# A one-core cross-attention and feed-forward kernel: the attention stage written out with paired score banks, shared rings and more DMA moves

## The reference, cut to what matters

```python
# B = 16 batches, 128 channels, T = 512; 8 heads of 16 channels, 8 of them rotary
x = x + tanh(g_xattn) * attention(layernorm(x), ctx)
x = x + tanh(g_ffn)   * ffn(layernorm(x))

def attention(x, c):
    q, k, v = Wq @ x + bq, Wk @ c + bk, Wv @ c + bv      # per batch, 128 x 512
    q, k = rope(q), rope(k)                              # first 8 channels of each head
    scores = einsum('bhqd,bhkd->bhqk', q, k) / sqrt(16)  # 512 x 512 for each head
    return Wo @ (softmax(scores) @ v) + bo

def ffn(x):                                              # weights packed in 4 bits with scales
    gate, up = x @ w_gu.T                                # 2 x 1408 wide
    y = (silu(gate) * up) @ w_down.T
    return y / rms(y)
```

## Time and profile before

| what | value |
|---|---|
| median of 3 executions | 930.14 us (928.13 to 931.05) |
| the profiled execution | 933.48 us, its span 931.6 us |
| mean granted TensorE clock in it | 0.94 of full |
| PE busy | 840.4 us (90%), 4134 matmuls |
| DVE busy | 557.3 us (60%) |
| ACT busy | 527.6 us (57%) |
| POOL busy | 211.5 us (23%) |
| DMA | 45439 packets, 74.36 MB |

### The profile page before, as it was taken

The page is one execution under the profiler, slowest core; times in us unless marked ns, Lnnn a source line. Parts: engine busy times, 40 slices in busy tenths (PEclk is TensorE's granted clock), DMA queues, the critical chain, the costliest instruction groups (busy, mean ns, idle before and its releaser), DMA issues. The chain is left out here.

```text
span 931.6 us, 13887 instructions
## 1 busy us (share of the span) xinstructions
PE 840.4 (90%) x4134; PEld 419.6 (45%) x4134; DVE 557.3 (60%) x1024; ACT 527.6 (57%) x991; POOL 211.5 (23%) x194
## 2 busy tenths in 40 slices
PE   4689989899898999998897579999999999999997
PEld 1333333333333333333321466666666666666664
DVE  5778988788988988889971872313231323232113
ACT  3228878788888888887874553325232523252223
POOL 5202434333434433341221940000000000000000
PEclk9559989999999999999966879999999999999999
DMA  6564453454554455443200101000200020000001
GB/s 187 147 184 124 127 151 112 146 160 130 154 153 123 152 147 164 129 133 86 70 24 12 57 1 46 1 0 22 69 1 1 15 75 0 0 11 34 1 1 45
DMA packets 45439, 74.36 MB, mean 80 GB/s; under 512 B 12122, under 2 KB 14426, under 8 KB 45402
## 3 DMA queue, kind: packets, MB, share of 16 engines
q1 hardware_dynamic: 45402, 73.90, 26.6%
HBM read 48.17 MB, written 25.17 MB: 79 GB/s over the span
## 5 line engine op out<-in xcount | busy, mean ns | idle before, releaser
L648 DVE TENSOR_REDUCE row_max<-s_ps 128x1 f32<-128x512 f32 x512 | 320.2, 680 | 54.1 <-PE s_ps L367 52.7
L540 ACT ACTIVATE probs<-st_ps 128x512 f32<-128x512 f32 x512 | 271.7, 599 | 97.3 <-PE st_ps L420 95.7
L367 PE MATMUL s_ps<-k_stack,q_stack 48*128 48x512 f32 x512 | 211.3, 489 | 24.9 <-DMA k_stack<-qk_scratch 21.4
L420 PE MATMUL st_ps<-q_stack,k_stack 50*128 50x512 f32 x512 | 197.2, 479 | 24.7 <-ACT probs L540 19.5
L367 PEld LDWEIGHTS s_ps<-k_stack,q_stack 48*128 48x128 f32 x512 | 91.7, 196 | 175.8 <-DVE row_max L648 126.8
L1123 PE MATMUL gu_ps<-x_head,gu_head 128*128 128x512 f32 x352 | 156.0, 443 | 0.0
L979 DVE TENSOR_TENSOR hidden<-gu_ps,silu 128x512 f32<-128x512 f32 x44 | 30.4, 690 | 202.6 <-ACT silu L1062 202.6
L388 PE MATMUL pv_ps<-probs,v_ones 128*32 128x512 f32 x1024 | 144.8, 640 | 0.0
L1062 ACT ACTIVATE silu<-gu_ps 128x512 f32<-128x512 f32 x44 | 26.3, 597 | 204.8 <-PE gu_ps L1126 204.7
L1124 PE MATMUL gu_ps<-x_rest,gu_head 128*128 128x512 f32 x352 | 138.9, 395 | 0.0
L420 PEld LDWEIGHTS st_ps<-q_stack,k_stack 50*128 50x128 f32 x512 | 82.9, 194 | 79.2 <-ACT probs L540 59.7
(11 more groups left out here) (131 smaller groups left out, 928.2 us busy)
## 6 DMA issues: line engine op xcount, KB each, us to landing
qk_scratch<-split SPq DMA_DIRECT2D x32, 512.0 KB, 4.5
k_stack<-qk_scratch SPq DMA_DIRECT2D x192, 64.0 KB, 2.2
q_stack<-qk_scratch SPq DMA_DIRECT2D x64, 128.0 KB, 2.5
xt<-x_dram SPq DMA_DIRECT2D x16, 256.0 KB, 2.9
ct<-ctx_dram SPq DMA_DIRECT2D x16, 256.0 KB, 3.7
cv<-ctx_dram SPq DMA_DIRECT2D x16, 256.0 KB, 2.8
q_stack<-qk_scratch SPq DMA_DIRECT2D x64, 64.0 KB, 2.5
x_res<-x_dram SPq DMA_DIRECT2D x16, 256.0 KB, 4.9
```

What stands on the lines that cost most here:

```text
L367: nc.tensor.matmul(s_ps[n % RING][:], q_stack[p][rows, head // 2, qt * P:(qt + 1) * P], k_stack[p][rows, head // 2, :], start=True, stop=T ...
L420: nc.tensor.matmul(st_ps[n % RING][:], k_stack[p][rows, head // 2, kt * P:(kt + 1) * P], q_stack[p][rows, head // 2, :], start=True, stop= ...
L540: nc.scalar.activation(probs[unit % 2][:, head % QUAD, kt % 2], st_ps[n % RING][:], ACT.Exp).then_inc(expd, 1)
L648: nc.vector.tensor_reduce(row_max[p][:, head % 2, head // 2, qt:qt + 1], s_ps[n % RING][:], AXIS_X, ALU.max).then_inc(maxed, 1)
```

## The change

The attention stage is written anew. All loops are unrolled, the weight stage of feed-forward too.

- **Scores:** the two heads at partition 0 and 64 write one double bank (`s_ps`, two of [128, 2, 512]), and one reduction takes both maxima, already negated. Both scores of a slot stand ahead of its two transposed scores.
- **Rings:** `misc_ps` is gone. Mixing (slot 1 of 16, for batch b-2), the rotary projection (slot 2) and the other (slot 5, both for b+3) take their turn in the three `st_ps` banks; the values projection takes a score bank (slot 8, after the scores). The exponentials write three `probs` tiles of one kt each; the values products stay in odd slots.
- **Maxima:** turned by a 32 x 32 transpose on DVE (`turn_max`), stored to DRAM and loaded into the stack in halves (`store_max`, `load_max`).
- **Rotary partners:** four SBUF to SBUF transfers (`swap_partners`) in place of the shuffle.
- **Sums:** two transfers gather the sums of a batch (`gather_sums`), DVE takes the reciprocal of a [128, 32] tile (`invert_sums`), and two transfers store it and one spreads it (`store_inverse`, `load_inverse`); four more put both quads into one tile (`merge_quads`), so that one multiplication on POOL scales all heads (`scale_heads`).
- **Moved:** the head parts go from ACT to DVE (`head_pass`, `head_rot`), `normalise` from DVE to POOL; x stays in eight tiles and ctx in four, so neither is loaded twice; `load_half` is four transfers from an image in DRAM that four stores for each half of the channels write. SP issues 38 transfers for a batch.
- **Feed-forward:** the unpacked 8-bit numbers are read as they are by `scale_tile`; the conversion to bf16 (`gu_vals`, `dn_vals`) is gone. The unpacking stands in the last step.

The diff, cut to its core:

```diff
-UNITS = 4
-RING = 3
+ST_BANKS, S_BANKS = 3, 2
+X_TILES, C_TILES, PROBS = 8, 4, 3
+MIX_AT, ROT_AT, PASS_AT, V_AT = 1, 2, 5, 8
...
-        s_ps = [ps(f"s_ps{r}", [P, T], F32) for r in range(RING)]
+        s_ps = [ps(f"s_ps{r}", [P, 2, T], F32) for r in range(S_BANKS)]
         pv_ps = ps("pv_ps", [P, T], F32)
-        misc_ps = ps("misc_ps", [P, T], F32)
...
+            def swap_partners(sp, n):
+                sp.wait_ge(st_read, ST_NO["rot", n] + 1)
+                if n:
+                    sp.wait_ge(rot_rest, n)
+                for at in range(0, P, 64):
+                    for to, source in ((at, at + 32), (at + 32, at)):
+                        sp.dma_start(swap[to:to + 32, :], proj[source:source + 32, 0, :]).then_inc(swapped, 16)
...
+            def load_max(sp, n, h):
+                sp.wait_ge(max_out[h], 16 * (n + 1))
+                for odd in two:
+                    row = STACK * odd + DATA_ROWS
+                    sp.dma_start(q_stack[n % 2][row:row + MAX_ROWS, columns(h), :].bitcast(F32).rearrange("r j t -> r (j t)"),
+                                 max_dram[n, h, :, odd].rearrange("r i e -> r (i e)")).then_inc(max_in[n % 2][h], 16)
...
+            def sync_step(sp, b):
+                nxt, proj_n = b + 1 < B, b + AHEAD_PROJ
+                if nxt:
+                    load_half(sp, b + 1, 1)
+                store_max(sp, b, 1)
+                if proj_n < B:
+                    swap_partners(sp, proj_n)
+                if b:
+                    gather_sums(sp, b - 1, 1)
+                    merge_quads(sp, b - 1)
+                load_max(sp, b, 1)
+                if b >= 2:
+                    store_x(sp, b - 2)
+                if b:
+                    store_inverse(sp, b - 1)
+                if proj_n < B:
+                    store_head(sp, proj_n, 1)
+                if b + 2 < B:
+                    load_half(sp, b + 2, 0)
+                if nxt:
+                    store_max(sp, b + 1, 0)
+                if b:
+                    load_inverse(sp, b - 1)
+                if proj_n < B:
+                    store_rest(sp, proj_n, 1)
+                if b + 5 < B:
+                    load_inputs(sp, b + 5)
+                if nxt:
+                    load_max(sp, b + 1, 0)
+                gather_sums(sp, b, 0)
+                if proj_n < B:
+                    store_head(sp, proj_n, 0)
+                    store_rest(sp, proj_n, 0)
...
+            def st_bank(pe, item):
+                n = ST_NO[item]
+                if n >= ST_BANKS:
+                    pe.wait_ge(st_read, n - ST_BANKS + 1)
+                return st_ps[n % ST_BANKS]
...
+            def tensor_step(pe, b):
+                for slot in range(SLOTS):
+                    if b + 1 < B:
+                        score(pe, b + 1, slot)
+                        if slot == V_AT:
                             project_v(pe, b + 1)
+                    weigh(pe, b, slot)
+                    if slot == MIX_AT and b >= 2:
+                        mix(pe, b - 2)
+                    if slot == ROT_AT and b + AHEAD_PROJ < B:
+                        project_rot(pe, b + AHEAD_PROJ)
+                    if slot == PASS_AT and b + AHEAD_PROJ < B:
+                        project_pass(pe, b + AHEAD_PROJ)
+                    if slot >= 3 and slot % 2:
+                        values(pe, b, slot // 2 - 1)
+                    elif slot == 1 and b:
+                        values(pe, b - 1, SPANS - 1)
...
+            def scalar_step(act, b):
+                for slot in range(SLOTS):
+                    for odd in two:
+                        exponential(act, b, 2 * slot + odd)
+                    if slot == MIX_AT and b >= 2:
+                        gate(act, b - 2)
+                    if slot == ROT_AT and b:
+                        values_out(act, b - 1, 1)
+                    if slot == ROT_AT and b + AHEAD_PROJ < B:
+                        bias_rot(act, b + AHEAD_PROJ)
+                    if slot == PASS_AT and b + AHEAD_PROJ < B:
+                        bias_pass(act, b + AHEAD_PROJ)
+                    if slot == 7 and b + 4 < B:
+                        inverse_dev(act, b + 4)
+                    if slot == 10:
+                        values_out(act, b, 0)
...
+            def maxima(dve, n, slot):
+                item = S_NO["score", n, slot]
+                j, qt = score_of(slot)
+                dve.wait_ge(s_full, item + 1)
+                nc.vector.tensor_reduce(neg_max[j // 2][:, :, j % 2, qt], s_ps[item % S_BANKS][:], AXIS_X, ALU.max,
+                                        negate=True).then_inc(s_read, 1)
...
+            def vector_step(dve, b):
+                proj_n = b + AHEAD_PROJ
+                for slot in range(SLOTS):
+                    if b + 1 < B:
+                        maxima(dve, b + 1, slot)
+                        if slot == V_AT:
+                            take_v(dve, b + 1)
...
+                    if slot == 0:
+                        turn_max(dve, b, 1)
+                    if slot == 3 and b + 4 < B:
+                        statistics(dve, b + 4)
+                    if slot == 6 and b:
+                        invert_sums(dve, b - 1)
+                    if slot == 7 and b + 1 < B:
+                        turn_max(dve, b + 1, 0)
+                    if slot == 7 and proj_n < B:
+                        head_pass(dve, proj_n)
+                    if slot == 11 and proj_n < B:
+                        head_rot(dve, proj_n)
...
-                for b in two:
-                    tensor_step(pe, b, b, B - 1 - b)
-                with pe.Fori(1, B // 2 - 2) as i:
-                    for p in two:
-                        tensor_step(pe, i * 2 + p, p, 4)
-                for b in range(B - 4, B):
-                    tensor_step(pe, b, b % 2, B - 1 - b)
+                for b in range(B):
+                    tensor_step(pe, b)
...
             def source(t):
+            parts = [keep[name][:].bitcast(FP8E3) for name in ("part_a", "part_b")]
```

1047 lines of the change are left out of this document (474 added, 573 removed).

## The result

The changed kernel takes 938.97 us (median of 4 executions, 936.54 to 945.54), the kernel before 929.22 us in the same comparison (928.13 to 931.05). The ratio is 1.0099, with a 95% interval of 1.0054 to 1.0144: slower, by 5 to 13 us. The forecast was 936 us with a range of 900 to 966. The profiled execution of the changed kernel took 936.54 us, that of before 933.48 us; what follows explains these two, 3.1 us apart. They lie 2 to 4 us from their medians, on opposite sides: the profiled execution of the changed kernel is the fastest of its four, that of before is slower than each of its four.

The account below looks back on a forecast made before the run. Bound: the loop PE, ACT, PE with PE's own work in series. Start -5.5, steps +8.4, loop turns -4.2, tail +7.5, feed-forward 0 sum to +6.2 us: 939.7 on the profiled scale, 936 us as a median, range 900 to 966.

Parts of the forecast that it names:

- The round as a loop PE, ACT, PE: Attention rounds: weight, exponential, fourth weight, values in series set the pace; a plain round costs 2.86 us for 2.72.
- The faster rival: Attention steps: time that ACT and DVE lose is in the path after all; 25.2 us a step, 902 us, chance 0.32.
- Products that share the ring: Mixing and pass in odd slots wait for the round's second exponential: rounds of 3.99 and 3.94 us.
- The sync queue: SP, 38 transfers a step for 31: second half's load_max arrives with 1.4 us to spare before slot 8, cost 0.
- The start: Before step 0: third projection 2.4 us later behind a queued partner swap; step 0 near 54.5, -5.5 us.
- The last step: Last attention step, batch 15: it has no scores in either kernel, so a difference of 0.
- two rivals: Range takes in the faster rival down to 900 and the queue's (late load_max, 960 us, chance 0.12) up to 966.
- The slower rival by the clock: Attention steps: the clock falls once in each step, 15 x 3 us, 981 us; chance 0.12.
- one of my signs of a wrong forecast: Mid-stage of attention: a granted clock below 1 would make the forecast wrong.
- The copies on DVE: Two head copies a batch on DVE: low end 0.36 us each; high end 1.61 us beside pool, 2.5 us more a step.
- Feed-forward: Weight stage reading 8-bit numbers directly: taken as 0, bounds -3 to +10 us.
- Tail: Last values to feed-forward: sums go by three DMA trips, 16.6 us for 9.1, +7.5 us, bounds +4 and +10.

Follow-up runs that it names:

- the woven one: Changed kernel with its scores put between the transposed scores: 949.33 us, ratio 1.0165; with the direct order for the maxima on SP as well, 930.65 us, ratio 0.9981.
- the run with the swap first: Changed kernel with only the second batch's swap of the rotary partners issued ahead of the first stack loads: 937.7 us, ratio 1.0114.
- the first combined kernel: Changed kernel with mixing and second projection in even slots, direct order for the maxima on SP, and repeated scores in the last step: 930.93 us, ratio 0.9977.

## Why the prediction was right, point by point

**The round as a loop PE, ACT, PE: right, and shown.** Every round came out within 0.04 us, and two runs test the mechanism and not only its size: 8.5 us less DVE work a step changed nothing, and an order that shortens only the way around the loop took 0.24 us from each plain round. The faster rival, that lighter ACT and DVE queues are in the path, is refuted for this order of instructions (by an experiment for DVE, by the rounds alone for ACT), and for DVE it returns in the woven one.

**Products that share the ring: right.** 3.96 and 3.91 us in odd slots as forecast, 3.33 in an even one.

**The sync queue: right in direction, with the wrong place and cause.** I gave the maxima of the second half 1.4 us to spare and checked issue times. Those of the first half were the late ones, in five of the steps, by 0.41 to 0.58 us, and not for the cost of the issues: the store issued at 220.76 us stood behind four stack loads, SP could issue the load that waits for it only at 226.45, behind x and ct, and PE had it 3.4 us later. In the step before, which had no stall, store and load went out 4.5 us apart for 5.7 (193.17 and 197.71), and the load 3.8 us ahead of the step's first scores for 2.5. Timelines of SP and PE in the changed kernel:

```profile
220.76 0.53 SPq L251 DMA_DIRECT2D max_scratch<-max_lines  x1
...
226.45 0.55 SPq L257 DMA_DIRECT2D q_stack<-max_scratch  x2
```

```profile
229.89 0.51 PE L431 MATMUL st_ps<-q_stack,k_stack 50*128 50x512 f32 x2 [0.41 <-DMA q_stack<-max_scratch]
```

The term that I set at 0 is +4.4 us over eleven batches, and some 1.6 us of it is a fall of the clock, told under the slower rival. The 1.9 us of landing that I used was a row of a kernel in which that transfer had little ahead of it. The second half's spare time was real and small: a round 0.24 us shorter used it up.

**The start: wrong by 7.4 us.** The term "2.4 us later" was 9.5 us; the place of the swap explains 7.8 of them, as the run with the swap first shows. (The written sum, 31.88 + 2.4 + 18.1 + 2.9, gives 55.3 us; 54.5 is what it gives from the first score, at 31.09.) The later steps of that term (18.1 us of reductions, 2.9 us of other work, against 21.3 from first score to first weight) held.

**The last step: wrong by 7.2 us, the other way.** I wrote that it has no scores in either kernel, and set 0. The clock was the difference, the row was there, and I did not cost it. The two errors cancel in the profiled pair to 0.2 us, so the sum (+6.2 for +3.2) looks better than it is, and that the median fell well inside the range is luck in part; the range, 900 to 966, was wide enough for two rivals. Since the executions of both kernels differ in this by up to 8 us, the 7.2 us is a property of two executions and not of the change; the range should have carried it.

**The slower rival by the clock: it did not come about in mid-stage, but for one fall.** From 95 to 450 us the changed kernel's mean granted clock is 0.995 with waits of 0.2 to 0.6 us in each round. It fell once, at 231.9 us, behind the stall of 0.41 us just shown, and came back at 235.3; the round from 228.98 took 6.18 us for 3.96:

```profile
231.57 1.80 PE L453 MATMUL st_ps<-heads_out,wo 128*128 128x512 f32 x2
233.30 1.93 PE L446 MATMUL pv_ps<-probs,v_ones 128*32 128x512 f32 x8
```

The late load was 0.6 of these 2.2 us and the clock 1.6; four other stalls of this kind, up to 0.58 us, had no fall behind them. A clock below 1 in mid-stage was one of my signs of a wrong forecast, and it came in this small form. By the Trainium skill, page "TensorE: Matmul & The Clock Gate", section "A second HAM failure mode: psum-queue depth-cycling", such small idles between groups make the clock swing; in these steps there was one such fall in 355 us. In the variants it fell behind single stalls of 0.65 to 3.7 us and in a step with little PE work, but the length of the one stall does not decide it: waits of 1.34 us (products in even slots) and 1.40 us (the first combined kernel) passed at the full clock.

**The copies on DVE: the low end was right.** 0.383 to 0.428 us for all 32. In 31 of them no pool instruction ran beside the copy; in one (78.11 us, 0.384 us) a pool instruction began 0.15 us before its end, and neither was longer than usual. So the price of a real clash is not shown here. **Feed-forward:** 0 forecast, -0.5 us measured, with 8-bit operands on pool.

**Tail: +7.5 forecast, +6.6 measured.** The three trips by DMA are the largest single loss of the profiled pair and were read from the earlier trace rows alone.

What stays open: why the first step runs at the lower clock for longer in some kernels than in others (last values of batch 0 between 90.6 and 100.1 us). The difference of the medians is 9.8 us against 3.1 in the profiled pair. At equal clock it is about 14 us, so the clocks can account for the gap; why they differ between the kernels is not shown beyond the last step.

## What to carry to other kernels

Write a beat down as the chain of waits that one buffer goes around, and cost an edit by whether it lies on that chain: 95 us less busy time on ACT and DVE brought nothing here, and 0.33 us in front of the first weight was worth 0.24 us a round. Small transfers that someone waits for belong ahead of large ones in the queue: what delayed them here was the transfers ahead of them and not the cost of their own issues. When a stretch of the profile before runs at a lower clock, give it a term and a range of its own, in both kernels. Before two profiles are compared, look at where each lies among its executions, and compare times at equal clock where there are enough of them.

## What the runs showed of the hardware

- A reduction of 128x1024 from two PSUM banks takes 1.216 us on DVE, of 128x512 in the same form 0.684 us.
- A transfer of 8 KB landed after 1.9 us in the kernel before, and PE had it 6.0 us after its issue behind 512 KB of loads.
- One wait of 0.41 us of PE was followed by the lower clock (changed kernel, 229.89 us), while waits of 1.34 and 1.40 us in two variants were not.
- Over 57 executions of the kernel before, 0.01 of mean granted clock goes with 6.3 us of its 930.
- The same instructions in the last step ran at 2.4 GHz in three of eight executions and at 1.2 GHz for all or part of it in the others; with repeated score products, 0.3 us a slot, all four executions looked at had the full clock.
- Two broadcasts of one number to 128 partitions took 2.79 and 3.02 us to issue on SP behind sixteen loads (8.36 and 11.19 us of the changed kernel), and 0.43 us each when third and fourth in the queue (kernel before).
